# Transposes of a group's own keys moved to the head of the next unit, and two context reloads cut into four parts each

## What is computed

```python
def _L0_xattn_ref(x, h_ctx_kv, wq, wk, wv, wo, wk_ctx, wv_ctx, q_norm_w, k_norm_w):
    q = (x @ wq).reshape(B, L, NUM_HEADS, HEAD_DIM)
    k = (x @ wk).reshape(B, L, NUM_KV_HEADS, HEAD_DIM)
    ...
    k = k * cos + rotate_half(k) * sin
    k_full = jnp.concatenate([k_ctx, k], axis=1)
    ...
    scores = jnp.einsum('blhd,bmhd->bhlm', q, k_full) * scale + mask
    probs = jax.nn.softmax(scores, axis=-1)
    out = jnp.einsum('bhlm,bmhd->blhd', probs, v_full)
    ...
    return out @ wo
```

## Time and profile before

| | before |
|---|---|
| median of 3 runs | 1298.2 us (1294.91 to 1299.37) |
| the profiled execution | 1299.34 us, span 1297.5 us |
| PE busy | 1193.7 us (92%) |
| DVE, ACT, POOL busy | 1015.4, 832.3, 790.8 us |
| granted TensorE clock, mean | 0.976 |
| from 127 to 1092 us (the attention groups): PE busy, clock | 925.57 of 965 us, 0.99 |

### The profile page before, as it was taken

The page is one execution under the profiler, slowest core; times in us unless marked ns, Lnnn a source line. Parts: engine busy times, 40 slices in busy tenths (PEclk is TensorE's granted clock), DMA queues, the critical chain, the costliest instruction groups (busy, mean ns, idle before and its releaser), DMA issues.

```text
span 1297.5 us, 30487 instructions
## 1 busy us (share of the span) xinstructions
PE 1193.7 (92%) x11547; PEld 893.8 (69%) x11547; DVE 1015.4 (78%) x1979; ACT 832.3 (64%) x1917; POOL 790.8 (61%) x1010
## 2 busy tenths in 40 slices
PE   4998699999999999999999999999999976777898
PEld 2544477877787777778777777777777765455557
DVE  6876768888688888788888878888888887776673
ACT  4755567776677676767677677777777644446431
POOL 2765386867668585857668595857768533761000
PEclk9998999999999999999999999999999998789999
DMA  8620067576867687695767677676778898000000
GB/s 286 201 82 15 18 137 163 129 159 134 187 135 154 143 148 149 128 209 130 159 132 152 145 148 147 133 160 139 151 145 153 161 193 222 1 1 1 1 1 33
DMA packets 507298, 164.94 MB, mean 127 GB/s; under 512 B 485488, under 2 KB 500352, under 8 KB 506896
## 3 DMA queue, kind: packets, MB, share of 16 engines
q1 hardware_dynamic: 506128, 159.57, 56.5%
q0 software_dynamic: 1024, 3.42, 1.0%
HBM read 33.05 MB, written 8.26 MB: 32 GB/s over the span
## 4 chain that ended last, share of the span: by engine, by line
PE 69%; DVE 16%; DMA 5%; POOL 3%; ACT 3%; issue 3%; SPq 2%; POOLq 0%; DVEq 0%; ACTq 0%
PE PS L1217 14%; PE PS L1219 13%; PE PS L1218 13%; PE PS L1369 7%; PE PS L1365 7%; PE PS L1366 7%; DVE mx L1722 5%; DVE pl L1742 3%; DMA pT_l<-pl 2%; DMA pT_h<-ph 2%; PE PS L1318 1%; PE PS L706 1%; PE PS L684 1%; DMA sin<-in_c_sin 1%; DVE f_s L1653 1%
## 5 line engine op out<-in xcount | busy, mean ns | idle before, releaser
L1722 DVE TENSOR_REDUCE mx<-PS 128x1 f32<-128x512 f32 (+2 forms) x512 | 296.5, 622 | 123.8 <-PE PS L1219 122.6
L1365 PE MATMUL PS<-v_h,pT_h 128*128 128x129 f16 (+1 forms) x1856 | 225.8, 222 | 9.9 <-DMA pT_h<-ph 9.9
L1959 POOL CAST ph<-pr_end 128x705 f16<-128x705 f32 (+1 forms) x128 | 109.9, 858 | 200.4 <-ACT pr_end L1517 200.4
L1366 PE MATMUL PS<-v_l,pT_h 128*128 128x128 f16 (+1 forms) x1856 | 225.8, 221 | 0.0
L1365 PEld LDWEIGHTS PS<-v_h,pT_h 128*128 128x128 f16 (+1 forms) x1856 | 182.7, 98 | 14.0 <-DMA pT_h<-ph 11.3
L1217 PE MATMUL PS<-kT_h,qT_h 128*128 128x512 f16 (+2 forms) x512 | 181.9, 355 | 7.6 <-ACT pr L1517 7.6
L1517 ACT ACTIVATE pr<-PS,nb 128x1024 f32<-128x1024 f32 x128 | 144.0, 1125 | 68.9 <-DVE nb L1730 68.9
L1366 PEld LDWEIGHTS PS<-v_l,pT_h 128*128 128x128 f16 (+1 forms) x1856 | 183.0, 99 | 2.4
L1218 PE MATMUL PS<-kT_l,qT_h 128*128 128x512 f16 (+2 forms) x512 | 181.0, 354 | 0.0
L1219 PE MATMUL PS<-kT_h,qT_l 128*128 128x512 f16 (+2 forms) x512 | 180.8, 353 | 0.0
L1742 DVE TENSOR_TENSOR pl<-pr,ph 128x1024 f16<-128x1024 f32 x128 | 169.3, 1322 | 0.0
(11 more groups left out here) (287 smaller groups left out, 2964.4 us busy)
## 6 DMA issues: line engine op xcount, KB each, us to landing
stage<-in_ctxT SPq DMA_DIRECT2D x8, 800.5 KB, 6.6
weights_kept<-relay SPq DMA_DIRECT2D x30, 128.0 KB, 2.3
relay<-in_w_lanes SPq DMA_DIRECT2D x14, 204.9 KB, 3.6
stage<-in_wq SPq DMA_DIRECT2D x4, 512.0 KB, 4.0
stage<-in_wo SPq DMA_DIRECT2D x4, 512.0 KB, 3.8
pT_h<-ph SPq DMA_TRANSPOSE x128, 3.6
pT_l<-pl SPq DMA_TRANSPOSE x128, 3.6
ctx_kept<-ctx_h SPq DMA_DIRECT2D x2, 800.5 KB, 8.1
```

The lines of the kernel that those rows point to most:

```text
L1365: mm(PS[:, OB, 0:DH + 1], pT_h[0:rows, slot, t, :], v_h[0:rows, par, v, :], start=t == 0, stop=False)
L1366: mm(PS[:, OB, 0:DH], pT_h[0:rows, slot, t, :], v_l[0:rows, par, v, :], start=False, stop=False)
L1722: dve.reduce_max(mx[:, c:c + 1], PS[:, c, 0:cols(u % LT, c)], AX_X).then_inc(mx_part, 1)
L1959: pool.tensor_copy(ph[:, slot, HALF:LAST + w], pr_end[:, 0:BANK + w]).then_inc(pool_hi, 1)
```

## The change

`("kq", 5)` leaves the end of unit 3 and becomes the first job of unit 4. The order of the list stays, and with it the PSUM banks and who waits for whom. The two context reloads are no longer issued in one go after groups 2 and 6: they come in four parts of 128 x 1601 f16 (400 KB), one in each of units 0 to 3 of groups 3 and 7, behind the transposes of that unit and, in unit 0, behind the lane load. The waits for `ctx_moved` count the new number of DMAs. The remaining edits of the diff (bank formulas written anew, a job kind "q" that no list contains) give the same banks and the same waits for these lists.

```diff
-           [("piece", 7), ("kq", 6), ("piece", 8), ("kq", 5)],
-           [("piece", 9), ("kq", 4), ("kq", 1)],
+           [("piece", 7), ("kq", 6), ("piece", 8)],
+           [("kq", 5), ("piece", 9), ("kq", 4), ("kq", 1)],
...
+                    if g in (KVH - 1, 2 * KVH - 1) and u < 2 * DC:
+                        bring_back(g // KVH, u)
...
-            def bring_back(slot, groups_done):
-
-                sp.wait_ge(pc_mm, NP * groups_done)
-                for k, t in enumerate((ctx_h, ctx_l)):
-                    sp.dma_start(t[:, slot, :, :].rearrange("p c n -> p (c n)"), kept[slot, k, :, :])\
-                      .then_inc(ctx_moved, 16)
+            def bring_back(slot, part):
+
+                if part == 0:
+                    sp.wait_ge(pc_mm, NP * KVH * (slot + 1))
+                t, c = (ctx_h, ctx_l)[part // DC], part % DC
+                sp.dma_start(t[:, slot, c, :], kept[slot, part // DC, :, c * SC:(c + 1) * SC]).then_inc(ctx_moved, 16)
...
-                if g in (KVH - 2, 2 * KVH - 2):
-                    bring_back(g // KVH, (g // KVH + 1) * KVH)
...
-                    pe.wait_ge(ctx_moved, 64 + 64 * (g // (2 * KVH)))
+                    pe.wait_ge(ctx_moved, 64 * max(1, g // KVH))
```

More of the change, by code:

```diff
@@ L75 @@
 JOB_LIST = [j for jobs in JOBS_AT for j in jobs]
-OUT_JOBS = [j for j in JOB_LIST if j[0] == "out"]
+RING = [j for j in JOB_LIST if j[0] != "q"]
 PREP_JOBS = [("piece", 0)] + [j for j in JOB_LIST if j[0] != "out"]
@@ L501, in build, with prep_user, job_bank @@
         PREP_BANKS = [TB, TB + 1, OB, XB]
+        prep_at = [sum(k != "q" for k, _ in PREP_JOBS[:n]) for n in range(len(PREP_JOBS))]
         def prep_bank(n):
-            return PREP_BANKS[n % len(PREP_BANKS)]
-        def job_bank(job):
-            return XBS[JOB_LIST.index(job) % len(XBS)]
+            return PREP_BANKS[prep_at[n] % len(PREP_BANKS)]
+        def prep_user(n):
+            if PREP_JOBS[n][0] == "q" or prep_at[n] < len(PREP_BANKS):
+                return None
+            return [j for j in PREP_JOBS if j[0] != "q"][prep_at[n] - len(PREP_BANKS)]
+        def job_bank(job, g):
+            if job[0] == "q":
+                return None
+            if g >= NG - 1:
+                return XBS[job[1] % LT]
+            return XBS[(g * len(RING) + RING.index(job)) % len(XBS)]
         def target(job, g):
@@ L519, in runs, with user_from, last_user @@
             return target(job, g) < NG
+        def user_from(at):
+            while at >= 0:
+                g, job = at // len(RING), RING[at % len(RING)]
+                if runs(job, g):
+                    return job, target(job, g)
+                at -= len(XBS)
+            return None
+        def last_user(bank):
+            end = (NG - 1) * len(RING)
+            return user_from(max(at for at in range(end - len(XBS), end) if XBS[at % len(XBS)] == bank))
         def bank_user(job, g):
             kind, i = job
+            if kind == "q":
+                return None
             if kind == "mean":
[L525 to L534, removed]
+                return last_user(MB) if i == 0 else (("mean", 0), g)
+            if g == NG - 1:
+                return last_user(XBS[i % LT]) if i < LT else (("out", i - LT), g - 1)
+            return user_from(g * len(RING) + RING.index(job) - len(XBS))
         def unit_no(g, u):
@@ L593, in run_job @@
             elif kind == "out":
-                kinds[kind](i, target(job, g), job_bank(job))
+                kinds[kind](i, target(job, g), job_bank(job, g))
             else:
                 to = target(job, g)
-                kinds[kind](i, to, to % 2, job_bank(job))
+                kinds[kind](i, to, to % 2, job_bank(job, g))
         def second(hf, j):
@@ L1410, in group @@
                         wait_bank(pe, ("out", 2), NG - 2)
-                        out_proj(0, NG - 1, job_bank(("out", 0)))
+                        out_proj(0, NG - 1, job_bank(("out", 0), NG))
                         pe.wait_ge(tw_const, 64)
@@ L1422, in _ @@
                     pe.wait_ge(l1_R, B)
-                if n >= len(PREP_BANKS):
-                    wait_bank(pe, PREP_JOBS[n - len(PREP_BANKS)], 0)
+                if prep_user(n):
+                    wait_bank(pe, prep_user(n), 0)
                 to = 1 if n == len(PREP_JOBS) - 1 else 0
@@ L1437, in _ @@
                 wait_bank(pe, *before)
-                out_proj(i, NG - 1, job_bank(("out", i)))
+                out_proj(i, NG - 1, job_bank(("out", i), NG))
             tail()
@@ L1573, in group @@
                         hi_part(0, 0, 1)
-                        out_hi_part(0, NG - 1, job_bank(("out", 0)))
+                        out_hi_part(0, NG - 1, job_bank(("out", 0), NG))
                     while todo:
@@ L1592, in _ @@
             copy_first(0, 1)
-            out_hi_part(1, NG - 1, job_bank(("out", 1)))
+            out_hi_part(1, NG - 1, job_bank(("out", 1), NG))
             tail()
@@ L1829, in group @@
                         lo_part(0, 0, 1)
-                        out_lo_part(0, NG - 1, job_bank(("out", 0)))
+                        out_lo_part(0, NG - 1, job_bank(("out", 0), NG))
                         quantise(0, True)
@@ L1881, in _ @@
             for i in range(1, 2 * LT):
-                out_lo_part(i, NG - 1, job_bank(("out", i)))
+                out_lo_part(i, NG - 1, job_bank(("out", i), NG))
             tail()
```

## The result

The changed kernel takes 1294.91 us in the median of 20 runs (1290.07 to 1301.07), the kernel before 1299.47 in 20 runs beside them (1294.27 to 1306.93). The ratio is 0.9955, 95% interval 0.9938 to 0.9972: faster by 5.8 us, between 3.6 and 8.1. The profiled execution has a span of 1292.7 us, 4.8 less than before, and took 1294.55 us.

What follows compares the result with a forecast made beforehand. PE was taken to bound the kernel, one matmul behind the other in the attention. The move's +4.8 us and the reloads' -6.9 gave -2.1, so 1296.1 us against the median 1298.2; range 1291 to 1305, the forecast's own 1293.5 to 1299.

Steps and rivals of the forecast that it cites:

- The class with the most chance, within 0.3%: Whole kernel: time within about 0.3% (3.9 us) of no change, chance 0.63; faster had 0.21, slower 0.16.
- The reloads, -6.9 us: Groups 3 and 7: reload parts behind each unit's transposes make none late, so all 6.9 us are gained.
- the 4.80: Extra length in us of the group behind the first reload, nearly PE's wait of 2.98 plus 1.7 lost to the clock.
- The wait moves from kq 5 to kq 1: Unit 4: kq 1 needs kq 5's bank and waits 0.84 us per group; kq 5's 0.29 or 0.62 goes.
- QK(6) not waiting for its exponential: QK(6) starts 1.6 us sooner, yet unit 5's exponential leaves its banks 0.53 us ahead, so no wait.
- +4.8 us for that move: Over 15 groups: 12.6 us of new wait at kq 1 for 7.8 us of old at kq 5.
- S: End of piece 8 on PE in group 7, taken as 599.63, from which the later starts were counted.
- DVE's lead over POOL: p_lo(5, 1) on DVE starts at S + 6.26, POOL's norm of kr at S + 6.46: DVE first by 0.20 us.
- Rival B: p_lo(5, 1) stalls behind POOL's norm, delaying kq 1 by 0.9 us a group, 13.5 in all: 1309.6 us; chance 0.11.
- Rival C: Kq 1 finds its bank free, no wait replaces the old: -14.7 us, time 1283.5; chance 0.12.
- Rival D: Reload parts still make a transpose late, PV(1) of groups 3 and 7 waits: 1297 to 1303 us; chance 0.13.

Runs made afterwards that it cites:

- reload_only: Changed kernel with kq 5 back at the end of unit 3, so only the reload in four parts: 1293.95 us, ratio 0.9954 to the kernel before.
- whole_unit1: Changed kernel with the reload uncut, two DMAs behind the transposes of unit 1 of groups 3 and 7: 1295.87 us, ratio 0.9976 to the kernel before.
- move_only: Kernel before with only kq 5 moved to unit 4, the reload as it was: 1302.58 us, ratio 1.0020 to the kernel before.
- dve_read512: Changed kernel with one more DVE maximum over 512 PSUM columns behind the four maxima of QK(6), ahead of p_lo(5, 1): 1329.99 us in one run.
- parts_unit0: Changed kernel with all four reload parts issued in unit 0, behind the lane load: 1298.15 us, ratio 0.9982 to the kernel before.
- three_jobs_late: Changed kernel with kq 1 first in unit 5 and ACT's and DVE's halves of the relayed piece one unit later: 1279.83 us, ratio 0.9850 to the kernel before.
- dve_late8: Changed kernel with eight DVE memsets of 128x6 behind the bias, ahead of p_lo(5, 1): 1296.00 us in one run.

## Why the prediction was right, and where it was off

The time, 1294.91, lies in the range and 1.2 us under the predicted 1296.1. But the kernel before came out higher in more runs, so the change is the fairer measure: predicted -2.1, measured -4.2 in the attention groups of the traces, -4.8 over the span and -5.8 by the ratio. The class with the most chance, within 0.3%, was the wrong one, narrowly: 0.45% faster.

- **The reloads, -6.9 us: right.** The traces have 4.7 + 2.0 in the changed kernel and the same in reload_only. The two causes named for the 4.80, the wait of 2.98 and the clock behind it, are both gone. How much of it is the place and how much the cutting was not said then: whole_unit1 shows that the place alone gives 5.8 of the 6.7; what the cutting alone would give in the old place stays open.
- **The wait moves from kq 5 to kq 1: right,** with DVE's subtraction as releaser, 0.05 us of hand-over, and QK(6) not waiting for its exponential. The start of kq 1 behind QK(6) was 4.50 us, predicted 4.48.
- **+4.8 us for that move: too big, and this is the term of the sum that failed.** It is "15 waits of 0.84 less 7.8 us". The 0.84 was worked out from the starts of matmuls, the 7.8 read from the idle times that the profile gives. Those count from the modelled end of the matmul before. Such a matmul of 256 columns is shown 0.27 us long, but the next one starts 0.11 behind it, as the row at 599.54 and the one at 599.65 above show. So each reported idle time leaves out 0.16 us. I took S as 599.92 - 0.29; it was 0.16 earlier, and the old waits were 7.8 + 15 x 0.16 = 10.2 us. Like for like the move costs 11.0 - 0.3 - 7.8 = 2.9 us by reported idle times, or 13.1 - 10.2 = 2.9 by starts. For the fourteen groups that lie between 215 and 1036 it is 12.2 - 9.7 = 2.5, and the table has 2.0 (move_only) and 2.3 (changed kernel less reload_only). With 2.9 the forecast would have been -4.0. The same 0.16 is in two margins of the prediction. QK(6) had 0.34 us behind its exponential and not 0.53: in group 7 the exponential ends at 595.74 and QK(6) starts at 596.08. And DVE's lead over POOL was larger, as follows.
- **Rival B: its mechanism is real, and it didn't happen.** The margin was 0.38 us and not 0.20: S, taken 0.16 too late, had put POOL's norm that much too early behind it (S + 6.46, measured S + 6.60). In every group p_lo(5, 1) was 0.69 long. dve_read512 shows the switch with 0.8 us a group, near the 0.9 predicted. What the prediction left out of B's price is the clock: its waits would have come to some 1.5 us, and behind 2.0 us it fell in half of the groups. Behind 1.45 us (dve_read512, last group, at 1060.92) it was 0.67, behind 1.67 (parts_unit0) 1.00, so B could have cost more than its 13.5. The rule of the Trainium skill (SBUF — State Buffer, section "Who interferes with whom"), that the operation which issues first holds the way for its whole length, is borne out here with the numbers above.
- **Rival C, no new wait: didn't happen with this change.** It took two more edits, kq 1 behind PV(4) and the relay copy a unit later. Its price of -14.7 had the same mistake in it: with the old waits at 10.2 and not 7.8 it is -17.1, or -16.6 for the fourteen groups from 215 to 1036, where three_jobs_late has -17.5.
- **Rival D: absent, with less margin than reckoned in one place** (1.1 us in group 7, predicted 2, and 2.8 in group 3).

What remains unexplained are 1.6 us between the -4.2 of the attention and the -5.8 of the ratio. 0.6 lie outside the attention in the profiled pair, where transfers of the preparation and of the last group differ from run to run by more than that. The rest is within the interval.

## What to carry to other kernels

Before you move a job away from a wait, ask how much work of the waiting engine stands between the job and the last reader of its buffer, in the new place as in the old: here the job found its wait again behind less cover, and a place with more cover, with the copy that then stood in the way moved too, was worth 13 us. A large transfer on the queue of a latency-bound one needn't be small; it must stand where the next transfer behind it has slack, and a wait of about 2 us that it causes can cost another 1.6 us or so in the clock. When a new wait is compared with an old one, take both from starts or both from the profile's idle times.

## What the runs showed of the hardware that wasn't expected

- The two operations of DVE and POOL on SBUF are decided wholly by their order: 1.50 and 1.04 us with POOL first by 0.07 to 0.09 us (dve_read512), 0.69 and 1.56 with DVE first by 0.03 (dve_late8), 0.69 and 1.36 by 0.22.
- Waits of PE of the same 1.98 to 2.00 us at the same place of the program are followed by the full clock in seven groups and by 0.66 over 5 us in seven. The length of the wait doesn't tell the two apart: it was 0.66 behind 2.98 us and 2.48 (move_only) at a reload, but 1.00 behind 2.38 (three_jobs_late, at 1022.90) and 2.52 (parts_unit0, at 163.14); and 1.00 behind 1.84 and 1.67 at a reload (move_only, parts_unit0), but 0.66 behind 1.86 (dve_late8, at 1030.66). What decides I can't tell.
- A DMA issue is not of fixed length for the issuing engine: a transpose behind four queued parts held SP 5.75 us, an undisturbed one 1.48 (both in group 3 of parts_unit0).
- Memsets of 128x6 behind each other take 0.01 us each (eight of them delayed kq 1 by 0.11 us a group), too little to delay an engine with.
